# Last attention of a four-layer model: another order of work inside each slot, and output products in two halves

## The reference, cut to what matters

```python
q = jnp.einsum('bpm,imh->bpih', x, W_Q) + b_Q
k = jnp.einsum('bpm,imh->bpih', x, W_K) + b_K
v = jnp.einsum('bpm,imh->bpih', x, W_V) + b_V
scores = jnp.einsum('bpih,bqih->bipq', q, k) / np.sqrt(64)
scores = jnp.where(causal, scores, -100000.0)
attn = jax.nn.softmax(scores, axis=-1)
z = jnp.einsum('bpih,biqp->bqih', v, attn)
out = jnp.einsum('bqih,ihm->bqm', z, W_O) + b_O
```

## Time and profile before

| | us |
|---|---|
| median of 3 runs (2262.9 to 2271.84) | 2263.21 |
| the profiled execution, its own time | 2263.8 |
| its span | 2262.0 |
| TensorE busy (share of the span) | 2022.2 (89%) |
| VectorE busy | 1403.7 (62%) |
| ScalarE busy | 1063.5 (47%) |
| GpSimd busy | 660.1 (29%) |

### The profile page before, as it was taken

One profiled execution on the slowest core, in us unless ns is written; L12 is line 12 of the kernel. 1 busy time (PEld: TensorE's weight loads), 2 busy tenths in 40 slices (PEclk: granted clock), 3 DMA queues, 4 the chain that ended last, 5 costly groups with the idle time before them and its releaser, 6 DMA issues. The chain is left out here.

```text
span 2262.0 us, 47075 instructions
## 1 busy us (share of the span) xinstructions
PE 2022.2 (89%) x18407; PEld 1391.1 (61%) x18407; DVE 1403.7 (62%) x3541; ACT 1063.5 (47%) x2552; POOL 660.1 (29%) x736
## 2 busy tenths in 40 slices
PE   4769999988879999698868898959999999999998
PEld 2546666657766677454546555755666666666565
DVE  4657777743555555456536886148767776777577
ACT  4436556542244454322234437346666666666222
POOL 4237920002110000103753006743333333333000
PEclk8769999998999999899985559979999999999999
DMA  1052030002010000241251004330000000000000
GB/s 48 19 43 15 2 39 2 2 17 57 13 56 1 1 1 1 66 145 21 39 141 38 2 22 132 41 103 7 1 1 1 2 1 1 1 1 1 6 15 19
DMA packets 118330, 63.65 MB, mean 28 GB/s; under 512 B 66232, under 2 KB 113632, under 8 KB 116960
## 3 DMA queue, kind: packets, MB, share of 16 engines
q1 hardware_dynamic: 106128, 51.85, 9.5%
q0 software_dynamic: 11264, 8.66, 2.7%
q10 hardware_dynamic: 720, 0.14, 0.0%
HBM read 36.76 MB, written 23.86 MB: 27 GB/s over the span
## 5 line engine op out<-in xcount | busy, mean ns | idle before, releaser
L3104 ACT ACTIVATE l_prob<-l_ps,l_neg_max 128x128 f32<-128x128 f32 (+1 forms) x512 | 208.6, 420 | 47.4 <-DVE l_neg_max L3203 42.5
L1684 ACT ACTIVATE l0a_prob<-l0a_pst 128x1024 f32<-128x1024 f32 x128 | 131.2, 1025 | 119.7 <-PE l0a_pst L1602 119.7
L2989 POOL TENSOR_TENSOR l_prob<-l_prob,l_total 128x256 f32<-128x256 f32 x128 | 78.5, 613 | 365.0 <-DVE l_total L3211 365.0
L1735 DVE TENSOR_REDUCE l0a_peak<-l0a_ps 128x4 f32<-128x1024 f32 x128 | 156.2, 1221 | 16.0 <-PE l0a_ps L1597 13.9
L1597 PE MATMUL l0a_ps<-l0a_k,l0a_q 32*128 32x256 f32 x1024 | 146.5, 406 | 3.0 <-ACT l0a_prob L1684 2.5
L680 ACT ACTIVATE l0e_hidden<-l0e_ph,l0f_b 128x512 f32<-128x512 f32 x128 | 87.8, 687 | 129.2 <-PE l0e_ph L591 129.2
L3199 DVE TENSOR_TENSOR l_ps<-l_ps,future 128x512 f32<-128x512 f32 x128 | 89.4, 698 | 93.3 <-PE l_ps L3035 93.1
L1602 PE MATMUL l0a_pst<-l0a_q,l0a_k 32*128 32x256 f32 x1024 | 145.8, 400 | 0.2 <-ACT l0a_prob L1684 0.2
L601 PEld LDWEIGHTS l0e_py<-l0f_w,l0e_hidden 128*128 128x128 f32 x1024 | 119.7, 192 | 35.0 <-ACT l0e_hidden L680 32.6
L2990 POOL TENSOR_TENSOR l_prob<-l_prob,l_total 128x512 f32<-128x512 f32 x128 | 133.2, 1040 | 0.0
L601 PE MATMUL l0e_py<-l0f_w,l0e_hidden 128*128 128x128 f32 x1024 | 129.8, 280 | 0.3 <-ACT l0e_hidden L680 0.3
(11 more groups left out here) (538 smaller groups left out, 4998.9 us busy)
## 6 DMA issues: line engine op xcount, KB each, us to landing
l_band<-zero SPq DMA_DIRECT2D x16, 272.0 KB, 6.7
x_tok<-in_x_dram SPq DMA_DIRECT2D x2, 2048.0 KB, 8.1
l2f_w<-in_L_ffn_w_dram SPq DMA_DIRECT2D x2, 2048.0 KB, 9.9
l_rows<-l_band SPq DMA_DIRECT2D x16, 256.0 KB, 3.7
l1f_w<-in_L_ffn_W_dram SPq DMA_DIRECT2D x3, 1024.0 KB, 12.2
gd_tri<-gp_tri SPq DMA_DIRECT2D x8, 256.0 KB, 2.0
l0f_w<-gd_tri SPq DMA_DIRECT2D x8, 256.0 KB, 10.6
gd_tri<-l0f_w SPq DMA_DIRECT2D x8, 256.0 KB, 8.1
```

Source lines behind the costliest of these rows:

```text
L1684: act.activation(prob[:, (n // 2) % 2, pair, :, :].rearrange("p g t s -> p g (t s)"), pst[:, :, :, :].rearrange("p g t s -> p g (t s)"), A ...
L1735: dve.tensor_reduce(to, ps[m % 2][:, :, :, :], AX.X, ALU.max, negate=True).then_inc(max_ready, 1)
L3104: act.activation(prob[:, m % 4, h, cols], ps[m % 2][:, h, cols], ACT.Exp, bias=neg_max[:, m % 4, h, t:t + 1], accum_out=total[:, m % 4, h, ...
```

## The change

1. Order on TensorE in a slot: scores, weighing, v or out job, transposes, qk job. The list of jobs of a slot is sorted so that qk comes last (in the very first slot it comes first).
2. VectorE saves k as soon as the qk job is done, and ScalarE's save of q now waits for that save. Before, it was the other way round.
3. The out job of a sequence becomes two jobs of 8 matmuls, each for 128 tokens, in the slots 3 and 5 of the next sequence (for the last sequence both in its slot 11). Each has its own save of 128 columns, where one save of 256 stood before.
4. ScalarE's order: save of z, save of v, exponentials, save of q. VectorE's order: mask, maxima, reciprocals, copy of the transposes, save of out, step of `choose`, save of k.
5. The projections read x from the stage's input `xnt` and no longer from `xs`; GpSimd's copies are gone.

```diff
-    PLAN = [("qk", n, n - 2) for n in range(PAIRS)] + [("v", n, n - 2) for n in range(4)] + [("out", 0, PAIRS + 4)]
+    PLAN = [("qk", n, n - 2) for n in range(PAIRS)] + [("v", n, n - 2) for n in range(4)] + [("out", n, PAIRS + 3 + 2 * n) for n in range(2)]
...
+            if b == NB - 1 and what == "out":
+                at = PAIRS + 3
             jobs.setdefault(b * PAIRS + at, []).append((what, b, n))
     last = max(jobs) + 1
+    for t in jobs:
+        jobs[t].sort(key=lambda j: (t > 0 and j[0] == "qk", j[0] != "qk"))
...
# TensorE, the out job
-                        for t in range(2):
-                            for g in range(PAIRS):
-                                ins = pe.matmul(px[:, t * P:(t + 1) * P], z[:, b % 2, g, t * P:(t + 1) * P], wo[:, g, :],
-                                                start=(g == 0), stop=(g == PAIRS - 1))
+                        for g in range(PAIRS):
+                            ins = pe.matmul(px[:, 0:P], z[:, b % 2, g, n * P:(n + 1) * P], wo[:, g, :],
+                                            start=(g == 0), stop=(g == PAIRS - 1))
...
# TensorE, the slot
                     if m < ALL:
                         scores(m)
-                    for j in now[0:1]:
-                        job(*j)
+                    if 0 <= m - 3 < ALL:
+                        weigh(m - 3)
+                    for j in now:
+                        if j[0] != "qk":
+                            job(*j)
                     if 0 <= m - 2 < ALL:
                         turn(m - 2)
-                    if 0 <= m - 3 < ALL:
-                        weigh(m - 3)
-                    for j in now[1:]:
-                        job(*j)
+                    for j in now:
+                        if j[0] == "qk":
+                            job(*j)
...
# ScalarE, save of q
                     if what == "qk":
+                        act.wait_ge(k_saved, by_dve[turn_of[what, b, n] + 1])
...
# VectorE, saves
-                        dve.wait_ge(job_saved, by_act[turn_of[what, b, n] + 1])
                         dve.tensor_scalar(k[:, b % 2, n, :], px[:, SEQ:], bk[:, n:n + 1], None, ALU.add).then_inc(k_saved, 1)
                     if what == "out":
-                        dve.tensor_tensor(st.s[:, bass.ds(i * (2 * NB) + 2 * b, 2), :],
-                                          px[:, 0:2 * P].rearrange("p (a b) -> p a b", a=2),
-                                          bo[:, :].unsqueeze(1).to_broadcast([P, 2, D]), ALU.add).then_inc(k_saved, 1)
+                        dve.tensor_tensor(st.s[:, 2 * b + n, :], px[:, 0:P], bo[:, :], ALU.add).then_inc(k_saved, 1)
...
# VectorE, the slot: after mask and maxima stood the first job's save
-                    for j in now[0:1]:
-                        save(*j)
...
                         dve.tensor_copy(turned[:, n % 2, :, :], pt[:, :, 0:3 * P]).then_inc(turned_saved, 1)
-                    for j in now[1:2]:
-                        save(*j)
-                    for j in now[2:]:
-                        save(*j)
+                    for j in now:
+                        if j[0] == "out":
+                            save(*j)
                     choose(m)
+                    for j in now:
+                        if j[0] == "qk":
+                            save(*j)
```

More of the change, by code:

```diff
@@ L2944, in layer3_attention @@
         bq8 = mem.sb("l3_bq8", [P, PAIRS])
-        xs = mem.sb("l3_x", [P, 2, SEQ])
         q = mem.sb("l3_q", [P, 2, PAIRS, SEQ])
@@ L2963, in layer3_attention @@
         px = mem.psum("l3_px", [P, 512])
-        names = ["l3_" + n for n in ("bias_ready", "x_ready", "job_ready", "job_saved", "k_saved", "scores_ready", "masked", "max_ready", "exp_ready",
+        names = ["l3_" + n for n in ("bias_ready", "job_ready", "job_saved", "k_saved", "scores_ready", "masked", "max_ready", "exp_ready",
                                      "recip_ready", "prob_ready", "turn_ready", "turned_saved", "z_ready", "z_saved", "logits_ready", "chance_ready",
@@ L2967, in layer3_attention, with inputs @@
         with phase(nc, names, BATCH // NB, spent=spent) as (block, i, sems):
-            (bias_ready, x_ready, job_ready, job_saved, k_saved, scores_ready, masked, max_ready, exp_ready, recip_ready, prob_ready, turn_ready,
+            (bias_ready, job_ready, job_saved, k_saved, scores_ready, masked, max_ready, exp_ready, recip_ready, prob_ready, turn_ready,
              turned_saved, z_ready, z_saved, logits_ready, chance_ready, choose_step) = sems
-            SLOTS = max(ALL + 4, last)
+            SLOTS = max(ALL + 3, last)
+            def inputs(b):
+                return st.xnt[:, b * SEQ:(b + 1) * SEQ]
             @block.sync
@@ L2978, in _ @@
             def _(pool):
[L2979 to L2985, removed]
                 for m in range(ALL):
@@ L2990, in _ @@
                     pool.tensor_tensor(far, far, total[:, m % 4, :, 1:2].to_broadcast([P, 2, 2 * P]), ALU.mult).then_inc(prob_ready, 1)
-                    if m % PAIRS == PAIRS - 1 and m // PAIRS + 2 < NB:
-                        copy_x(m // PAIRS + 2)
             @block.tensor
@@ L3005, in job @@
                         pe.wait_ge(z_saved, PAIRS * (b + 1))
-                        for t in range(2):
-                            for g in range(PAIRS):
-                                ins = pe.matmul(px[:, t * P:(t + 1) * P], z[:, b % 2, g, t * P:(t + 1) * P], wo[:, g, :],
-                                                start=(g == 0), stop=(g == PAIRS - 1))
-                    else:
-                        pe.wait_ge(x_ready, b + 1)
-                        x = xs[:, b % 2, :]
+                        for g in range(PAIRS):
+                            ins = pe.matmul(px[:, 0:P], z[:, b % 2, g, n * P:(n + 1) * P], wo[:, g, :],
+                                            start=(g == 0), stop=(g == PAIRS - 1))
+                    x = inputs(b)
                     if what == "qk":
@@ L3110, in save_z @@
                     if b >= 2 and n == 0:
-                        act.wait_ge(job_ready, turn_of["out", b - 2, 0] + 1)
+                        act.wait_ge(job_ready, turn_of["out", b - 2, 1] + 1)
                     act.activation(z[:, b % 2, n, :], pz[:, 0:SEQ], ACT.Identity, bias=bv[:, n:n + 1]).then_inc(z_saved, 1)
@@ L3119, in _ @@
                         now = now[1:]
-                    for j in now[0:1]:
-                        if j[0] != "out":
+                    if 0 <= m - 3 < ALL:
+                        save_z(m - 3)
+                    for j in now:
+                        if j[0] == "v":
                             save(*j)
```

## The result

The changed kernel takes 2306.64 us, the median of 4 runs (2303.99 to 2308.91); the kernel before took 2264.82 beside it (4 runs, 2262.9 to 2271.84). The ratio is 1.0176, 95% interval 1.0155 to 1.0197. It is 42 us slower; I had forecast 2310 us, +46.

What follows compares the result with a forecast made beforehand. The prediction took TensorE's pace as the bound. Sequences +41, choose +4 and the end +1 made +46 us on the profiled 2263.8, so 2310 us, range 2288 to 2328.

Steps and rivals of the forecast that it cites:

- scores to weighing: Start of each slot on TensorE: weighing follows scores after 0.85 us, with ends of 0.65 and 1.06.
- plain slot: Slot with neither v nor out job: 3.36 us against 3.37 before, no stall.
- v slot: Slot with a v job: 4.54 us, qk waiting 0.22 for the save of v behind the transposes.
- out slot: Slot with a half output job, two of eight: 6.72 us, of which 1.5 us is a new stall.
- end: End of the stage: two half jobs with a save between and weighing ahead of the transposes cost +1 us.
- The stall in the out slots: Before qk in out slots: VectorE copies the transposes, then saves out, so TensorE waits 1.5 us.
- Saves of k first: VectorE's k save before ScalarE's q save: no gain in the stream; with the missing x copy, 0 overall.
- The steps of choose: VectorE's steps ahead of the save of k, slots 3 to 17: +4 us, ends 0 and +12.
- my sign of waits before their v jobs: Sign to look for in the changed profile: slots 3 to 17 show waits before v jobs.
- turning hides the release of l_px: Rival, v and out slots: transposes may hide the saves; sequence 34.4 us, total 2251; 4%.
- The clock: Rival, out slots: stalls lower TensorE's clock, 3 us more in each of 30, 2400 us; 5%.
- VectorE was no bound: Rival: VectorE becomes the bound, plain and out slots lose 0.2 each, another +12, 2322 us; 10%.

Runs made afterwards that it cites:

- e1_save_first: Changed kernel with VectorE saving the output products before copying the transposes: 2261.29 us, 0.997 of the kernel before; a sequence 35.21 us.
- e2_one_out: Changed kernel with one output job of 16 matmuls in slot 4 and one save of 256 columns: 2280.21 us, a sequence 36.77 us.
- e5_quarter_v: Changed kernel saving only 128 of each 512 columns of v, the rest a constant: v slots 4.23 us, a sequence 37.06 us.
- e3_q_first: Changed kernel with the old save order, ScalarE saving q before VectorE saves k: 2323.89 us, a sequence 39.90 us.

## Why the prediction was right

The steps as I put them, and what was measured, per piece and in the stage:

| step | forecast | measured |
|---|---|---|
| scores to weighing | 0.85 | 0.85 |
| plain slot | 3.36 | 3.33 |
| v slot | 4.54 | 4.53 |
| out slot | 6.72 | 6.74 |
| sequence | 38.3 | 38.25 |
| 15 sequences | +41 | +38.5 (from the second on, 2.65 each; the last, counted to its last scores only, 0.8 less; one of the kernel before was 0.35 longer) |
| choose, first sequences, start | +4 | +1.5 (0.8 in the first sequence, 1.4 in the second, 0.7 less ahead of the first scores) |
| end | +1 | +2.9 from the last scores, 1.4 of it clock |

- *The stall in the out slots* was the cause, at its size: copy 0.96 and save 0.28 behind the transposes. From the start of the transposes to qk it takes 2.15 where it takes 0.65 in `e1_save_first`, so each stall is 1.5 us; the 1.34 of the view counts only from the modelled end of the transposes. `e1_save_first` shows it by taking it away, `e2_one_out` by halving its number.
- *The v slot* was right as a sum by luck, with two errors inside that cancel. Qk to scores was taken as 1.06; it is 0.96 when nothing waits and its weights are loaded ahead (`e5_quarter_v`). So the bare slot is 4.23 and not 4.32, and the wait costs 0.30 and not 0.22. The 0.1 that I read as the price of one change of array shape was half of it: four changes against three make 4.43 against 4.23.
- *Saves of k first* I put at 0 "in the stream", for the reason that both saves are needed anyway. The reason is wrong: with q first, behind the exponentials, a sequence takes 1.65 us more and the stage 650.4 against 627.9 (`e3_q_first`). The sum came out because my slots had been worked out with k first. The 0.7 us ahead of the first scores was put down to this and to the missing copy of x; no run separates the two.
- *The steps of choose* were mis-sized. By slots, the changed kernel lost 3.4 us to them and the kernel before 1.3, so +2 where I had +4. The changed kernel lost 1.4 in v slots (6 and 7 of the first sequence), not 4.5 in nine of them, and 2.0 in the two out slots of the second, as forecast; the other v slots of slots 3 to 17 took 4.53 to 4.56, so my sign of waits before their v jobs did not come. I had taken each step at some 1.2 to 1.5 us. That was the time of one that ran beside GpSimd's multiplication. In the kernel before, that multiplication was

```profile
1567.70 1.04 POOL L2990 TENSOR_TENSOR l_prob<-l_prob,l_total 128x512 f32<-128x512 f32 x1
```

and the step of the earlier trace rows began 0.11 behind its start. In the changed kernel four of the six slots with such comparisons run them mostly behind the multiplication, and the same instruction (128x128) takes a third (a row of the groups by shape):

```profile
L3150 DVE TENSOR_TENSOR l2f_w<-l2f_w 128x128 f32<-128x128 f32 x1 | 0.4, 400 | 0.0
```

The two that still ran beside it took 1.06 and 1.23. They stand in the plain slots just ahead of the two out slots that lost 1.0 each.
- *Rivals.* That turning hides the release of l_px was false, as forecast; it becomes true in the out slots as soon as the save precedes the copy (`e1_save_first`). The clock stayed at 1.00 from the second sequence to the last scores, with 1.34 us of idle time twice in 38; it fell only at the stage's end, in one profile. VectorE was no bound (26 of 38 us).
- *The last terms* came near the forecast by luck in part: choose and start were 2.5 too high, the end 1.9 too low, and 1.4 of that end belongs to one execution.

## What to carry to other kernels

When several jobs share one buffer, count the time from a job's last instruction to the release of the buffer on the engine that releases it, with everything that stands ahead of the release in that engine's order. Putting other work between a job and the next one, so that it hides the release, is worth nothing if the other engine must first clean up after that work and only then releases the buffer. Here the transposes were meant to hide the save of the output products, but VectorE copied the transposes first. Look for this before the change is judged as a whole: three moved lines turned 1.8% slower into 0.3% faster.

## What the runs showed that I had not expected

- An instruction of VectorE with both inputs in SBUF took 1.18 us beside a GpSimd multiplication and 0.40 apart from it. The Trainium skill, "SBUF — State Buffer", section on who interferes with whom, says that such an instruction contends with a GpSimd instruction that reads SBUF; the rows agree, but no run here was made to separate the two engines.
- A qk job that has to wait takes 0.1 us more to the next scores (1.06 against 0.96); its weights are then not loaded ahead.
- The Trainium skill's rule that a change of the tiling mode drains TensorE ("TensorEngine Tiling (Array Packing)", Key Properties) agrees with v slots of 4.43 with four changes and 4.23 with three, no wait in either; 0.2 us, of which the page gives no figure. No run here tells the drain apart from the weights that are not loaded ahead across such a change.
